# Graph attention kernel on one core: 22 of 782 edge tiles gathered as x rows in stage 1 and projected in the loop, the q bias by matmul, reciprocal roots in 12 steps

## What is computed

```python
q, k, v = (feat @ W.T + b for each of Wq, Wk, Wv)            # 6250 x 256, as 8 heads of 32
score = clip(sum_d q[dst] * k[src] / sqrt(32), -10, 10)      # 100000 x 8
alpha = exp(score - max over dst) / (sum over dst)
wv    = segment_sum(alpha * v[src], dst)                     # 6250 x 256
x2    = feat + wv @ Wp.T + bp
h     = layernorm(x2, g, b);  h = gelu(h @ W1.T + b1) @ W2.T + b2
out   = layernorm(feat + x2 + h)
```

## Time and profile before

| | us |
|---|---|
| median of 3 runs | 1587.08 (1579.13 to 1596.17) |
| the profiled execution | 1577.4 |
| its span, first to last instruction | 1573.7 |
| PE busy | 1073.0 (68%) |
| DVE busy | 1008.3 (64%) |
| POOL busy | 745.6 (47%) |
| ACT busy | 522.9 (33%) |
| mean granted TensorE clock | 0.805 of full |

### The profile page before, as it was taken

The page is one execution under the profiler, slowest core; times in us unless marked ns, Lnnn a source line. Parts: engine busy times, 40 slices in busy tenths (PEclk is TensorE's granted clock), DMA queues, the critical chain, the costliest instruction groups (busy, mean ns, idle before and its releaser), DMA issues.

```text
span 1573.7 us, 23781 instructions
## 1 busy us (share of the span) xinstructions
PE 1073.0 (68%) x5894; PEld 686.1 (44%) x5894; DVE 1008.3 (64%) x1770; ACT 522.9 (33%) x1357; POOL 745.6 (47%) x800
## 2 busy tenths in 40 slices
PE   8923467676667766677667676657767776766887
PEld 7811234453444443344444344334444444444566
DVE  6825567576656675576666666667566667566783
ACT  2211123333324333334324333324324333323443
POOL 0075555555545555545545545545455555445400
PEclk9955577787878787788877878788778887688899
DMA  8876766666656655656756656656665766656610
GB/s 285 271 226 181 242 203 196 205 182 187 210 173 192 208 174 183 194 165 197 210 162 198 210 165 197 201 181 190 192 186 178 214 190 190 194 176 194 187 50 22
DMA packets 156217, 297.43 MB, mean 189 GB/s; under 512 B 32087, under 2 KB 92597, under 8 KB 156086
## 3 DMA queue, kind: packets, MB, share of 16 engines
q0 software_dynamic: 62560, 205.05, 43.3%
q1 hardware_dynamic: 93526, 91.14, 18.5%
HBM read 261.75 MB, written 34.34 MB: 188 GB/s over the span
## 4 chain that ended last, share of the span: by engine, by line
DVE 27%; issue 25%; another core or an unknown queue 25%; PE 18%; ACT 2%; DVEq 1%; DMA 1%; POOL 0%; ACTq 0%; SPq 0%; POOLq 0%
DVE score L1372 9%; DVE ev L1385 8%; PE quad L762 4%; PE bank L395 3%; PE bank L415 2%; DVE prod L1365 2%; DVE stats L425 2%; PE bank L367 1%; PE bank L832 1%; PE quad L823 1%; DVE onehot L1353 1%; PE bank L812 1%; PE bank L844 1%; PE quad L395 1%
## 5 line engine op out<-in xcount | busy, mean ns | idle before, releaser
L334 POOL DMA_INDIRECT kv<-kv_rows,src_sb x782 | 742.7, 950 | 741.3 <-DVE ev L1385 404.3
L1365 DVE TENSOR_TENSOR prod<-kv,quad 128x1024 f32<-128x1024 f32 x196 | 239.2, 1221 | 322.8 <-remote 294.0
L823 PE MATMUL quad<-qwin,onehotT 32*128 32x256 f32 x1568 | 168.2, 503 | 236.2 <-DVE prod L1365 164.7
L395 PE MATMUL bank<-hT,w_sb 128*128 128x256 f32 x736 | 223.4, 457 | 52.1 <-ACT hid L403 34.0
L1372 DVE TENSOR_REDUCE score<-prod 128x32 f32<-128x1024 f32 x196 | 237.7, 1213 | 1.7
L1385 DVE TENSOR_TENSOR ev<-kv,bank 128x1024 f32<-128x1024 f32 x196 | 237.8, 1213 | 0.5 <-ACT ev L1046 0.5
L823 PEld LDWEIGHTS quad<-qwin,onehotT 32*128 32x128 f32 x1568 | 73.2, 217 | 337.7 <-issue 199.7
L395 PEld LDWEIGHTS bank<-hT,w_sb 128*128 128x128 f32 x736 | 168.4, 234 | 101.8 <-issue 37.6
L415 PE MATMUL bank<-w_sb,hid 128*128 128x256 f32 x736 | 197.8, 424 | 0.0
L832 PE MATMUL bank<-ev,onehot 128*32 128x264 f32 x1568 | 146.2, 445 | 60.3 <-issue 33.0
L812 PE MATMUL bank<-staged,place 128*128 128x264 f32 x196 | 95.8, 581 | 133.7 <-ACT staged L1054 90.5
(11 more groups left out here) (115 smaller groups left out, 1058.7 us busy)
## 6 DMA issues: line engine op xcount, KB each, us to landing
dst_rows<-edge_dstT SPq DMA_DIRECT2D x50, 256.0 KB
qwin<-q_rows SPq DMA_DIRECT2D x392, 32.0 KB
kv<-kv_rows,src_sb POOLq DMA_INDIRECT x782
kv_rows<-kv_out SPq DMA_DIRECT2D x24, 512.0 KB, 3.1
agg_rows<-acc_sb SPq DMA_DIRECT2D x98, 82.5 KB
xT_sb<-xT SPq DMA_DIRECT2D x25, 256.0 KB, 3.7
xq_sb<-xT SPq DMA_DIRECT2D x25, 256.0 KB
agg_in<-agg_rows SPq DMA_DIRECT2D x24, 264.0 KB
```

The lines of the kernel that those rows point to most:

```text
L334: return nc.gpsimd.indirect_dma_start(out=rows, out_offset=None, in_=kv_dram, in_offset=bass.IndirectOffsetOnAxis(ap=index, axis=0))
L395: last = nc.tensor.matmul(bank[:, j * SB:(j + 1) * SB], w1_sb[:, k * HIDDEN + f * P:k * HIDDEN + (f + 1) * P], hT[:, k], start=(k == 0), s ...
L823: last = nc.tensor.matmul(quad[:, i, 0:C], onehotT[rows, slot // 2, cols], qwin[rows, slot // 2], start=True, stop=True)
L1365: nc.vector.tensor_tensor(prod[:, slot % 2].rearrange("p (i c) -> p i c", c=C), kv[:, slot, :, 0:C], quad[:, :, 0:C], ALU.mult).then_inc(s ...
```

## The change

- `X_TILES`: tile 3 of slots 5 and 7 in turns 0 and 1, and of slot 7 in turns 6 to 23, 22 tiles in all. Their k and v are not gathered in stage 2. Instead GpSimd gathers the x rows of their source nodes (1 KB a row, half of k and v) in stage 1, one tile for each unit that is projected, into `xg`.
- In stage 2, for the x tile of slot 7: ScalarE copies the rows to `distance` (i = 3), TensorE transposes (i = 4), ScalarE copies to `xgT`, TensorE multiplies with the fp32 weights and the k and v bias (i = 5, `project_x`, bank7), ScalarE copies the result to `kv` (i = 6), and the product of slot 7 waits for that copy. For slot 5 all is two steps earlier, with the last copy at i = 3.
- `q_bias` goes from VectorE. The bias enters bank6 by `bias_matmul`, ScalarE copies at i = 2 (`copy_q`). `project_q` reads `wqkv_in`, and `wq_sb` with its load goes.
- `inverse_roots`: one Newton step, then one step of a higher order in five instructions; 12 waits in place of 13.
- The split of the biases (now 7 x 256 wide) goes from turn 0 to units 14, 16 and 18 of stage 1. `prod`, `staged`, `clipped` and `score` lie where stage 1's buffers lay.
- SyncE's `load_sources` has a gate increment after each of its four waits.

```diff
 def inverse_roots(tiles, step):
...
-            for _ in range(NEWTON):
-                step(nc.vector.tensor_tensor(y2, y, y, ALU.mult))
-                step(nc.vector.tensor_tensor(y2, y2, half, ALU.mult))
-                step(nc.vector.scalar_tensor_tensor(y, y2, 1.5, y, ALU.add, ALU.mult))
+            step(nc.vector.tensor_tensor(t, y, y, ALU.mult))
+            step(nc.vector.tensor_tensor(t, t, half, ALU.mult))
+            step(nc.vector.scalar_tensor_tensor(y, t, 1.5, y, ALU.add, ALU.mult))
+            step(nc.vector.tensor_tensor(t, y, y, ALU.mult))
+            step(nc.vector.tensor_tensor(r, t, v, ALU.mult))
+            step(nc.vector.tensor_scalar(t, r, 0.375, -1.25, ALU.mult, ALU.add))
+            step(nc.vector.tensor_tensor(t, t, r, ALU.mult))
+            step(nc.vector.scalar_tensor_tensor(y, t, 1.875, y, ALU.add, ALU.mult))
...
+def x_slots(turn):
+    if not isinstance(turn, int) or LOOP_FROM <= turn < LOOP_FROM + 2 * LOOPED:
+        return (7,)
+    return (5, 7) if turn < 2 else ()
...
 # SyncE
             def load_sources(turn, parity, t):
                 for b in range(4):
-                    sp.wait_ge(s_kv[4 * t + b], 64 * (turn + 1))
-                sp.sem_inc(s_gate_sp, 1)
+                    sp.wait_ge(s_kv[4 * t + b], kv_done(turn, 4 * t + b))
+                    sp.sem_inc(s_gate_sp, 1)
...
 # GpSimd
+            pool.wait_ge(s_xsrc, 16)
+            for k in range(len(X_TILES)):
+                pool.wait_ge(s_mm, min(4 + 2 * k, KV_HALVES))
+                nc.gpsimd.indirect_dma_start(
+                    out=xg[:, k, :], out_offset=None, in_=x,
+                    in_offset=bass.IndirectOffsetOnAxis(ap=x_src_sb[:, k:k + 1], axis=0)).then_inc(s_xg, 16)
...
-                    for t in range(gathered(n)):
+                    for t in range(X_TILE if i in x_slots(turn) else gathered(n)):
...
 # TensorE
                 for a in range(2):
+                    bias_matmul(bank6[:, a * C:(a + 1) * C], 6 * C)
                     for k in range(KC):
                         last = nc.tensor.matmul(bank6[:, a * C:(a + 1) * C], xq_sb[:, k, a * P:(a + 1) * P],
-                                                wq_sb[:, k * C:(k + 1) * C], start=(k == 0), stop=(k == KC - 1))
+                                                wqkv_in[:, k, 0:C], start=False, stop=(k == KC - 1))
                 last.then_inc(f_qm, 1)
+
+            def transpose_x(turn, i):
+                if exists(turn - 2, SUPERBLOCKS):
+                    pe.wait_ge(f_ev, 4 * (turn - 1))
+                k = x_index(turn, i)
+                pe.wait_ge(s_xrow, k + 1)
+                for j in range(KC):
+                    last = nc.tensor.transpose(bank7[:, j * P:(j + 1) * P], distance[:, j * P:(j + 1) * P], ident[:])
+                last.then_inc(s_xgT, 1)
+
+            def project_x(turn, i):
+                pe.wait_ge(s_xgTc, x_index(turn, i) + 1)
+                bias_matmul(bank7[:], 4 * C)
+                for j in range(KC):
+                    last = nc.tensor.matmul(bank7[:], xgT[:, j], wqkv_in[:, j, C:3 * C], start=False, stop=(j == KC - 1))
+                last.then_inc(s_xkvm, 1)
...
 # TensorE, node_steps, behind ffn1 and ahead of project_q
+                if i + 3 in x_slots(turn):
+                    transpose_x(turn, i + 3)
+                if i + 2 in x_slots(turn):
+                    project_x(turn, i + 2)
...
 # ScalarE, node_steps, ahead of everything else in it
+                for j in x_slots(turn):
+                    if i == X_COPIED[j]:
+                        copy_x_kv(turn, j)
+                if i == 2 and exists(turn, Q_UNITS - EARLY_Q):
+                    copy_q(turn)
+                if i + 4 in x_slots(turn):
+                    copy_x_rows(turn, i + 4)
+                if i + 3 in x_slots(turn):
+                    copy_x_columns(turn, i + 3)
...
+            def copy_x_kv(turn, i):
+                act.wait_ge(s_xkvm, x_index(turn, i) + 1)
+                if exists(turn - 1, TURNS):
+                    act.wait_ge(s_ev, SLOTS * (turn - 1) + i + 1)
+                nc.scalar.activation(kv[:, i, X_TILE, :], bank7[:], ACT.Copy).then_inc(s_xkv, 1)
...
 # VectorE
             def products(n, slot, turn):
-                dve.wait_ge(s_kv[slot], 64 * turn + 16 * gathered(n))
+                dve.wait_ge(s_kv[slot], kv_done(turn, slot) - 16 * (TILES - gathered(n)))
+                if slot in x_slots(turn):
+                    dve.wait_ge(s_xkv, x_index(turn, slot) + 1)
...
-            def q_bias(turn):
-                dve.wait_ge(f_qm, turn + 1)
-                if exists(turn - 1, Q_UNITS - EARLY_Q):
-                    dve.wait_ge(f_qst, 16 * turn)
-                nc.vector.tensor_tensor(q_next[:], bank6[:].rearrange("p (a c) -> p a c", c=C),
-                                        bq_sb[:].unsqueeze(1).broadcast_to([P, 2, C]), ALU.add).then_inc(f_qb, 1)
```

More of the change, by code:

```diff
@@ L33 @@
 CHECK_STEPS = 13
+BIAS_SPLIT = (14, 16, 18)
+X_TILE = TILES - 1
+X_COPIED = {5: 3, 7: 6}
 EX_COL = 0
@@ L47, in configure @@
     TURNS = -(-(BATCHES + 3) // SLOTS)
+    LOOPED = max(TURNS - 7, 0) // 2
+    LOOP_FROM = 6 if LOOPED else TURNS - 1
+    X_TILES = [(turn, i) for turn in range(TURNS) for i in x_slots(turn)]
     EDGE_COLS = BATCHES * TILES
@@ L63, in kv_halves, with x_index, kv_done, gnn_program @@
     return 1 if u * SB + P >= NODES else 2
+def x_slots(turn):
+    if not isinstance(turn, int) or LOOP_FROM <= turn < LOOP_FROM + 2 * LOOPED:
+        return (7,)
+    return (5, 7) if turn < 2 else ()
+def x_index(turn, i):
+    return X_TILES.index((turn, i)) if isinstance(turn, int) else turn + (X_TILES.index((LOOP_FROM, i)) - LOOP_FROM)
+def kv_done(turn, i):
+    if isinstance(turn, int):
+        return sum(16 * (TILES - (i in x_slots(u))) for u in range(turn + 1))
+    each = 16 * (TILES - (i in x_slots(turn)))
+    return turn * each + (kv_done(LOOP_FROM, i) - LOOP_FROM * each)
 configure(6250, 100000)
-def gnn_program(nc, xT, x, w_qkvT, b_kv, b_q, wpT, b_rows, ln_gb, w1T, b1, w2T, edge_src, edge_dst, edge_dstT,
+def gnn_program(nc, xT, x, x_src, w_qkvT, b_kv, b_q, wpT, b_rows, ln_gb, w1T, b1, w2T, edge_src, edge_dst, edge_dstT,
                 bases, out):
@@ L110, in gnn_program @@
         bases_sb = sb("bases_sb", [P, PAIRS + 1], i32)
-        dst_sb = sb("dst_sb", [P, EDGE_COLS], i32)
         dloc = sb("dloc", [P, EDGE_COLS])
-        beyond = sb("beyond", [P, EDGE_COLS])
         base_rise = sb("base_rise", [P, PAIRS])
         carry_all = sb("carry_all", [P, PAIRS])
-        parts = sb("parts", [P, 3, PAIR_TILES + 1])
         margins = sb("margins", [P, 6])
@@ L154, in gnn_program @@
         g_onehot = sb("g_onehot", [P, P])
-        wqkv_in = sb("wqkv_in", [P, KC, 3 * C], f32, early)
+        bias_in = sb("bias_in", [1, 7 * C], f32, early)
+        bias_lo = sb("bias_lo", [1, 7 * C], f32r, early)
+        dst_sb = sb("dst_sb", [P, EDGE_COLS], i32, early)
+        beyond = sb("beyond", [P, EDGE_COLS], f32, early)
+        parts = sb("parts", [P, 3, PAIR_TILES + 1], f32, early)
+        tile_start = sb("tile_start", [P, 2, TILES], f32, early)
+        x_src_sb = sb("x_src_sb", [P, len(X_TILES)], i32, early)
         wqkv_sb = sb("wqkv_sb", [P, 2, KC, 3 * C], f32r, early)
@@ L162, in gnn_program @@
         q_out = sb("q_out", [P, EARLY_Q, 2, C], f32, early)
+        bq_sb = sb("bq_sb", [P, C], f32, early)
         early.close()
         kv = sb("kv", [P, SLOTS, TILES, 2 * C])
+        prod = sb("prod", [P, 2, TILES * C])
+        staged = sb("staged", [P, 2, ACC])
+        clipped = sb("clipped", [P, 2, TILES * H])
+        score = sb("score", [P, 2, TILES * H])
         quad = ctx.enter_context(nc.psum_tensor("quad", [P, 4, 512], f32))
@@ L288, in turns @@
         def turns(eng, body):
-            looped = max(TURNS - 7, 0) // 2
-            first = 6 if looped else TURNS - 1
-            for turn in range(first):
+            for turn in range(LOOP_FROM):
                 body(turn, turn // 2, turn % 2)
-            if looped:
-                with eng.Fori(3, 3 + looped) as r:
+            if LOOPED:
+                with eng.Fori(LOOP_FROM // 2, LOOP_FROM // 2 + LOOPED) as r:
                     body(2 * r, r, 0)
                     body(2 * r + 1, r, 1)
-            for turn in range(first + 2 * looped, TURNS):
+            for turn in range(LOOP_FROM + 2 * LOOPED, TURNS):
                 body(turn, turn // 2, turn % 2)
@@ L570, in load_weights @@
             def load_weights(turn, i):
-                if (turn, i) == (0, 6):
-                    sp.wait_ge(s_bias, 2)
-                    sp.dma_start(bias_rows[1:2].bitcast(f32), bias_lo[:].bitcast(f32)).then_inc(s_lo, 16)
                 if (turn, i) == (0, 5):
@@ L1113, in node_steps @@
                 ends = isinstance(turn, int) and turn == TURNS - 1
-                if i == 4 and isinstance(turn, int) and turn == 0:
-                    split_biases()
+                for j in x_slots(turn):
```

(2 more changed lines are left out.)

85 lines of the change are left out of this document (51 added, 34 removed).

## The result

| | before | after |
|---|---|---|
| median of 4 runs, us | 1587.15 (1579.13 to 1596.17) | 1538.71 (1536.64 to 1542.43) |
| ratio | | 0.9696 [0.9641, 0.9751] |
| profiled execution: time, span | 1577.4, 1573.7 | 1542.4, 1540.6 |
| up to the first product of turn 0 | 89.4 | 89.2 |
| turns 0 and 1 | 127.1 | 124.4 |

What follows compares the result with a forecast made beforehand. GpSimd's gather bursts were taken to bound the kernel, delaying TensorE's signals. Gathers -27.5, stage 1 +2, projection +7, others 0 and roots -5.6 summed to -24 us: 1563 us from the median 1587.1, range 1540 to 1592.

Steps and rivals of the forecast that it cites:

- What bounds the kernel: Stage 2: TensorE's signals are seen late while GpSimd issues many gathers in a row, so burst length lies on the path.
- 22 x 1.25 = -27.5: Stage 2: each of 22 gathers fewer takes 1.25 us out of a burst, -27.5 us; bounds nothing and -40.
- R3: Rival, stage 2: each gather is worth its whole share of the turn, 1.83 us; -44 in sum, 1543 us; chance 0.12.
- Bursts of 7 or 11 where 8 or 12 stood: Sign of being right, loop: slot 7's gathers come out of bursts that end in a stall, shortening them by one.
- The lag of 1.7 us behind a burst: Sign of being right, stage 2: products still start 1.7 us behind a burst's end.
- Turns of 57.6 us: Sign of being right: loop turns of about 57.6 us (58.7 - 1.25 - 0.2 + 0.4).
- x rows in stage 1, +2: Stage 1: 22 more gathers of x rows fit nearly into free DMA time, +2 us; bounds 0 and +10.
- Projection, +7: Loop: TensorE's projection of the x tile is mostly hidden, +0.4 us a turn, +7 us; bounds 0 and +52.
- R2: Rival, loop: the projection's new TensorE signals are seen late, 2.5 us a turn, +45, 1608 us; chance 0.10.
- R1: Rival, loop: TensorE takes the gain back, projection costing 26 us in place of 7, 1582 us; chance 0.20.
- Roots, -5.6: At i = 6 and in the tail: 28 calls one step shorter, 0.2 us each where nothing stalls, -5.6 us.
- q bias, 0: Stage 2, i = 2: q bias off VectorE, 24 x 0.69 us before a stall, taken as 0; bound -16.5.

Runs made afterwards that it cites:

- g1: Kernel before, but from turn 1 on ScalarE's plain loads of fixed rows replace the gathers, without their wait for `ev`; 1178.20 us, ratio 0.7497.
- e3: Kernel after without transposes, projection and copies for the x tiles; their 22 gathers stay out, k and v stale; 1525.50 us, ratio 0.9635.
- g2: e2 without tile 3 of slots 1, 3, 5 and 7 in the loop, 72 gathers fewer, nothing in their place; 1438.87 us, ratio 0.9164.
- e4: Kernel before, each gather from turn 1 on fetching 1 KB a row instead of 2 KB, same count; 1583.79 us, ratio 1.0004.
- e2: Kernel after without any x tile: all 782 gathers in stage 2, none in stage 1, no projection; 1582.19 us, ratio 0.9990.
- e1: Kernel before with only the new `inverse_roots`; 1589.18 us, ratio 1.0023.
- e5 to e8: e2 without tile 3 of slot 7; 3; 3 and 7; 1, 3, 5 and 7 in the loop; short condition, ratios 0.9613, 0.9571, 0.9575, 0.9549.
- h1 to h3: First three kernels of e5 to e8 repeated unchanged, again in the short condition; ratios 0.9624, 0.9602, 0.9606.

## Why the prediction was wrong

*What bounds the kernel: right for the long condition, and now shown rather than argued.* Without GpSimd's gathers nearly the same work takes a quarter less (g1). With fewer of them it takes less (e3, g2). With half of their bytes it takes the same (e4). That TensorE's signals are seen late is still a reading of the timelines; no run shows what holds them up.

*The step that failed: 22 x 1.25 = -27.5.* I had both numbers, 1.25 us of burst and 58.7 / 32 = 1.83 of turn, and took the first as the value and the second as a bound. The model behind the first was that what lies between bursts, 1.7 us of lag and two or three batches of VectorE, is a fixed price. The runs showed that it isn't: GpSimd's wait for `ev` shrinks with the count, and the turn is 1.79 to 1.85 us a gather in six kernels. Measured, the term is -56 +/- 11 for these 22 (e2 and e3), 28 more than was put down, and 1.81 +/- 0.16 us each for 72 (g2). R3, to which I gave 0.12, comes nearest in its sum, -44 against -48, but partly by luck. Its -40 for the gathers is too small for these 22, and it had -5.6 for roots that show no gain and nothing for a projection that cost some 10; the errors nearly cancel. What it has right is that a gather is worth more than its 1.25 us of issue, and its 1.83 is the price of the 72.

*Bursts of 7 or 11 where 8 or 12 stood: half right.* Over the loop, the kernel before has 45 bursts of 4, 35 of 8, three each of 7 and 12 and one of 3, beside a few others; the one after has 43 of 4, 33 of 8, 13 of 3 and 7 of 7. Most of the gathers taken thus came out of a burst of 4, which becomes one of 3. Of the 52 bursts of 4 in the whole kernel before only 10 end in a stall of VectorE above 2 us, of the 41 of 8 it is 33. The term was thus argued from the wrong bursts as well. Nor do all stalls end with a burst: of VectorE's 460 us in stalls above 2 us during stage 2, 318 end within 3 us behind one. The lag of 1.7 us behind a burst was right (1.68 in turn 14).

*Turns of 57.6 us*: 56.38 measured.

*x rows in stage 1, +2*: about 0. The DMA share rose to 1.01 and 0.94, and the first gather of stage 2 came 0.3 us earlier.

*Projection, +7*: 10 +/- 12, or 0.76 a turn where 0.4 was taken. The single times were right (0.63 and 1.99 us). The working said that the 0.81 us of idle ahead of `q_rows` would go, and it went; the 1.9 us of slack behind it did not: in turn 14 `q_rows` ends at 948.26 and its product starts at 950.39. The product's 22.5 us of waiting for the copied k and v, seven times, is R2's place, but each wait is at most 5.2 us and the total price leaves no room for R2's 45 us. R1 wanted 26 us and is outside too, by the interval (10 + 12), if only just.

*Roots, -5.6*: 0.2% +/- 0.7% the other way (e1). This term was charged as path time because "nothing stalls" at i = 6; if the gathers pace the whole turn, VectorE has slack there too, but that is argued, since the interval would hold the 5.6. *q bias, 0*: right in the long condition as far as 0.5% can tell (e2, 0.9990).

*What stays open.* It isn't known why 22 gathers were worth 2.56 +/- 0.5 us each and 72 only 1.81 +/- 0.16: the intervals nearly touch, so it may be no more than scatter, or it is their place in slot 7, which the runs e5 to e8 and h1 to h3 could not test. Nor do the runs show what holds up TensorE's signals while GpSimd issues, where most of the 0.57 us comes from by which a gather's share exceeds its issue, whether the low clock of the long condition costs time of its own beside the stalls, or what puts the chip in one or the other condition.

## What to carry to other kernels

When a ring of buffers is paced by the engine that fills it, an item's own duration is not what taking it out is worth: the waits between the bursts shrank with the count here. The turn's time over its count of items, 1.83 us against 1.25, was right for 72 gathers and still too little for 22 of them, so such a price has to be measured. Idle time ahead of one instruction is not a price either: ahead of VectorE's product it grew by 94 us while the kernel fell by 48, because the instruction that used to take 85 of it was gone. And time the kernel before beside every series of runs: here the same edit got its gain from the gathers in one condition and mostly from other parts in the other, and absolute times of two series differ by a quarter.

## What the hardware showed beyond that

- One and the same kernel took 1571 to 1587 us in some series and 1167 to 1172 in others. The mean granted TensorE clock of its runs was 0.80 to 0.81 in the first and 0.90 to 0.92 in the second. The traces kept of the second, of other kernels, have none of the "remote" waits ahead of the product; a gather's record and its issue gap are 0.95 and 0.30 us in both.
- In the long condition 750 gathers replaced by plain loads of nearly the same bytes gave a ratio of 0.7497; in the short one the same edit gave 0.9905.
- Halving each gathered row from 2 KB to 1 KB changed nothing (1.0004, +/- 0.7%), neither in time nor in the issue gap.
- In the long condition the lag behind a burst that ends in a stall grows with its length, from a median of 1.64 us behind 7 gathers to 2.59 behind 12.
